# Attention phase of a float32 layer: scores of two blocks issued together, transposed probabilities kept in the score banks, and reordered first and last steps of the phase

## The reference, cut to what matters

```python
x = x + attn_ref(layernorm(x), mem, ...)        # x: 8192 rows of 256
x = x + ffn_ref(layernorm(x), ...)              # routed experts
# attn_ref, in front of each sequence 64 rows of mem:
q, k, v = x_in @ wq.T, x_in @ wk.T, x_in @ wv.T          # 4 heads of 64
mask = (j <= i) & (j > i - 128)                          # window of 128 keys
attn = softmax(where(mask, q @ k.T / 8, -1e30));  out_swa = (attn @ v) @ wo.T
grads = grad of 0.5 * sum((mlp(w1, b1, w2, b2, x_in) - out_swa) ** 2)
# one step on w1, b1, w2, b2; out = sigmoid(..) * out_swa + sigmoid(..) * mlp(new, x_in)
```

## Time and profile before

| | us |
| --- | --- |
| median of 3 runs | 2390.28 (2389.48 to 2391.47) |
| the profiled execution, device time | 2382.2 |
| its span in the profile | 2380.4 |
| PE busy | 2330.7 (98%) |
| DVE busy | 1691.1 (71%) |
| ACT busy | 1608.3 (68%) |
| POOL busy | 1394.6 (59%) |

### The profile page before, as it was taken

How to read it: one execution, slowest core, us unless ns; L and a number is a source line. 1 busy time by engine, 2 the same in 40 slices (tenths; PEclk the granted TensorE clock), 3 DMA queues, 4 the chain that set the end, 5 groups by cost and what they waited for, 6 DMA issues and landing times. The chain is left out here.

```text
span 2380.4 us, 39979 instructions
## 1 busy us (share of the span) xinstructions
PE 2330.7 (98%) x14822; PEld 2078.7 (87%) x14822; DVE 1691.1 (71%) x3666; ACT 1608.3 (68%) x2457; POOL 1394.6 (59%) x1000
## 2 busy tenths in 40 slices
PE   7999999899999999999999999999999999999998
PEld 6888888788888888888888978888888789999998
DVE  7787786666666666666666677777777867777776
ACT  4778878757777777777777647777777645554453
POOL 3566566656667766666666744666666553343433
PEclk9999999999999999999999999999999999999999
DMA  4222221442323322322233332332222165555551
GB/s 130 83 84 77 89 72 63 175 158 63 67 67 67 76 63 63 63 67 63 63 63 71 77 107 76 105 105 96 91 84 83 32 165 140 140 151 146 143 141 58
DMA packets 295394, 221.74 MB, mean 93 GB/s; under 512 B 189282, under 2 KB 262023, under 8 KB 295072
## 3 DMA queue, kind: packets, MB, share of 16 engines
q1 hardware_dynamic: 281376, 188.74, 29.3%
q0 software_dynamic: 13824, 30.44, 4.3%
HBM read 113.30 MB, written 72.12 MB: 78 GB/s over the span
## 5 line engine op out<-in xcount | busy, mean ns | idle before, releaser
L2742 ACT ACTIVATE e_hf<-e_ps_z,e_b 128x640 f32<-128x640 f32 x128 | 101.8, 795 | 211.9 <-PE e_ps_z L105 211.4
L2466 POOL TENSOR_TENSOR m_hl<-m_hf,m_hh 128x512 fp32r<-128x512 f32 x112 | 159.5, 1450 | 100.6 <-ACT m_hh L2067 100.4
L2870 POOL DMA_INDIRECT out<-e_ys,slot_token x80 | 83.2, 1040 | 216.6 <-DVE e_ys L2821 211.1
L105 PE MATMUL e_ps_y<-r_w_h,e_hl 128*128 128x256 f32 x640 | 180.7, 282 | 0.0
L105 PE MATMUL e_ps_y<-r_w_l,e_hh 128*128 128x256 f32 x640 | 179.3, 280 | 0.0
L105 PE MATMUL e_ps_y<-r_w_h,e_hh 128*128 128x256 f32 x640 | 179.0, 280 | 0.0
L914 POOL DMA_INDIRECT xbuf_d<-xn,scatter_rows x128 | 142.0, 1109 | 60.4 <-issue 35.4
L1650 POOL TENSOR_TENSOR halves_l<-hT_full,halves_h 128x512 fp32r<-128x512 f32 x120 | 153.5, 1301 | 38.7 <-ACT halves_h L1308 38.7
L771 POOL TENSOR_TENSOR prob<-prob,softmax_small 128x1024 f32<-128x1024 f32 x65 | 123.1, 1894 | 71.8 <-DVE softmax_small L689 71.8
L105 PE MATMUL e_ps_z<-slotsT_h,w_l 128*128 128x320 f32 x512 | 158.6, 310 | 0.7 <-DVE slotsT_l L2799 0.7
L105 PE MATMUL e_ps_z<-slotsT_l,w_h 128*128 128x320 f32 x512 | 158.5, 310 | 0.0
(11 more groups left out here) (359 smaller groups left out, 8961.2 us busy)
## 6 DMA issues: line engine op xcount, KB each, us to landing
shared_xT<-xT_d SPq DMA_DIRECT2D x64, 256.0 KB, 4.6
new_w1T<-in_W SPq DMA_DIRECT2D x16, 1024.0 KB
new_w2T<-in_W SPq DMA_DIRECT2D x16, 1024.0 KB, 5.7
xbuf_d<-new_w1T SPq DMA_DIRECT2D x16, 650.0 KB, 8.1
shared_x<-in_x SPq DMA_DIRECT2D x16, 512.0 KB, 4.1
xn_d<-xn SPq DMA_DIRECT2D x32, 256.0 KB, 2.5
xT_d<-shared_xT SPq DMA_DIRECT2D x32, 256.0 KB, 2.6
oT_d<-shared_oT SPq DMA_DIRECT2D x32, 256.0 KB, 2.6
```

What stands on the lines that cost most here:

```text
L105: i = e.matmul(out, a, b, start=first and not onto and n == 0, stop=last and n == len(terms) - 1, skip_group_check=onto)
L2466: e.tensor_tensor(hl[:, t, 0:N], hf[(HC * C + t) % NZ][:, 0:N], hh[:, t, 0:N], ALU.subtract).then_inc(*h_low(C, t))
L2742: e.activation(hf[(HC * i + t) % NHF][:].rearrange("p (s n) -> p s n", s=2), ps_z[t % 2][:, :, 0:HALF], ACTF.Relu, bias=b1[:, i % E, t:t + ...
L2870: e.indirect_dma_start(io["out"], bass.IndirectOffsetOnAxis(ap=token[i % 2][:, b:b + 1], axis=0), ys[:, b], None, bounds_check=NT - 1, oob ...
```

## The change

Six edits, all of order and place; the numbers computed are the same.

1. **Scores in pairs.** In an even turn PE issues `scores(a)` and `scores(a + 1)` one behind the other, in an odd turn none.
2. **Banks.** There are two sets of score banks, `ps_sets[g % 2]`, and the transposed probabilities of block g are written over the scores of block g + 2, in the same set; `ps_probT` is gone. So `transpose_p(g)` waits for the maxima of g + 2, and `scores(g)` for `rest_pt(g - 4)`.
3. **Order on ACT and DVE.** `soft(a)` goes ahead of the roundings and of `round_pt(a - 2)` (in turns 0, 4, 8, ... ahead of `round_pt` alone). DVE takes the maxima of an odd block in the even turn before it, and those of an even block at the end of the odd turn before it, behind `rest_pt`. In turns 0, 4, 8, ... the roundings of x come before the maxima of the odd block. POOL normalises `a - 1` ahead of the rests of x.
4. **Turns without early projections**: PE does `attend(a - 3)` first, then `transpose_p(a - 2)`.
5. **Opening.** The six projections of group 1 leave `opening()` and go, two in a turn, into turns -1, 0 and 1.
6. **The phase's end.** ACT rounds the first block of x for the gradient phase and loads the sigmoid's table ahead of the last output copies, DVE takes that block's rest; in the gradient phase the first seed goes ahead of `round_xT(0)`, the third block's x is rounded alone and early (`round_xT2`), and PE's first two products wait for no rest.

```diff
     G, j = a // GRP + 2, a % GRP
+    second = parts(1, 2 * a + 4) + parts(1, 2 * a + 5) if a < 2 else []
     if a < 0 or G >= NGRP:
-        return [], []
-    return parts(G, 2 * j) + (parts(G, 1) if j == 0 else []), parts(G, 2 * j + 1) if j else []
+        return [], second
+    return parts(G, 2 * j) + (parts(G, 1) if j == 0 else []), second + (parts(G, 2 * j + 1) if j else [])
...
         for n in range(2, 8):
-            out += parts(G, n)
+            out += parts(G, n) if G != 1 else []
...
-        ps_s = ps("ps_scores", [P, 2, 2, 2 * P])
-        ps_pt = ps("ps_probT", [P, 2, HEADS, P])
+        ps_sets = [ps(f"ps_scores{i}", [P, 2, 2, 2 * P]) for i in range(2)]
...
+        def scores_of(g):
+            return ps_sets[g % 2]
+
+        def probT_of(g):
+            return ps_sets[g % 2][:].rearrange("p b c (h q) -> p b (c h) q", q=P)
...
-                pe.wait_ge(*top_made.at(g - 1))
+                pe.wait_ge(*top_made.at(g - 2))
+                pe.wait_ge(*pt_low.at(g - 4))
+                ps_s = scores_of(g)
...
-                p = pr[g % NPR]
+                p, ps_pt = pr[g % NPR], probT_of(g)
                 pe.wait_ge(*prob_made.at(g))
-                pe.wait_ge(*pt_low.at(g - 1))
+                pe.wait_ge(*top_made.at(g + 2))
+                pe.wait_ge(*pt_low.at(g - 2))
...
-                if a in turns:
+                if a == MEM_BLOCK:
                     scores(a)
+                elif a % 2 == 0 and a in turns:
+                    scores(a)
+                    scores(a + 1)
                 for kind, *key in early:
                     do[kind](*key)
-                if a - 2 in turns:
+                if early and a - 2 in turns:
                     transpose_p(a - 2)
                 if a - 3 in turns and a - 3 < last:
                     attend(a - 3)
+                if not early and a - 2 in turns:
+                    transpose_p(a - 2)
...
+            def round_first():
+                act.wait_ge(*next_xT.at(0))
+                act.wait_ge(*score_done.at(NBLK - 9))
+                e.activation(firsth, shared.pair_xT(0)[:, :, 0:P], ACTF.Copy).then_inc(*first_high(0))
+
+            def load_sigmoid():
+                act.wait_ge(*half_set.at(0))
+                e.activation(spare[:], neg_half[:, 0:1], ACTF.Sigmoid)
...
+                if a % GRP and a in turns:
+                    soft(a)
                 for kind, *key in early:
                     do[kind](*key)
+                if a % GRP == 0 and a in turns:
+                    soft(a)
                 if a - 2 in turns:
                     round_pt(a - 2)
-                if a in turns:
-                    soft(a)
                 if a - 3 in turns and a - 3 < last:
                     copy_av(a - 3)
                 if a - 3 == last:
                     round_last_av()
+                    round_first()
+                    load_sigmoid()
                 for kind, *key in late + output_at(a):
                     do[kind](*key)
                 if a in w1_turns:
                     round_w1(w1_turns.index(a))
...
                 early, late = steps_at(a)
-                if a in turns:
+                if a == MEM_BLOCK:
                     maxima(a)
-                if a - 1 in turns:
+                if a % 2 and a - 1 in turns:
                     invert(a - 1)
-                for kind, *key in early:
-                    do[kind](*key)
+                if a % GRP == 0:
+                    for kind, *key in early:
+                        do[kind](*key)
+                if a % 2 == 0 and a + 1 in turns:
+                    maxima(a + 1)
+                if a % GRP:
+                    for kind, *key in early:
+                        do[kind](*key)
                 if a - 2 in turns:
                     rest_pt(a - 2)
-                for kind, *key in late:
-                    do[kind](*key)
+                if a % GRP != 1:
+                    for kind, *key in late:
+                        do[kind](*key)
                 if 0 <= a and G < NGRP and j == 0:
                     norm_stats(G, 0)
                     norm_stats(G, 1)
                 elif 0 <= a and G < NGRP and j < 3:
                     norm_apply(G, j - 1)
+                if a % 2 and a in turns:
+                    invert(a)
+                if a % 2 and a + 1 in turns:
+                    maxima(a + 1)
+                if a % GRP == 1:
+                    for kind, *key in late:
+                        do[kind](*key)
...
             rest_last_av()
+            dve.wait_ge(*first_high.at(0))
+            e.tensor_tensor(firstl, shared.pair_xT(0)[:, :, 0:P], firsth, ALU.subtract)
...
+                if a - 1 in turns:
+                    normalise(a - 1)
                 for kind, *key in early + late:
                     if kind == "x":
                         rest_x(*key)
-                if a - 1 in turns:
-                    normalise(a - 1)
...
+                h, l = (firsth, firstl) if g == 0 else (xTh[:, :, block[b]], xTl[:, :, block[b]])
                 for i, hc in enumerate(cols):
                     pe.wait_ge(*seeded.at(g, i))
-                    pe.wait_ge(*xT_low.at(p))
-                    matmul_split(e, bank("z", g, i)[:], [(xTh[:, k, block[b]], xTl[:, k, block[b]]) for k in range(KC)],
+                    if g:
+                        pe.wait_ge(*(xT2_low.at(0) if g == 2 else xT_low.at(p)))
+                    matmul_split(e, bank("z", g, i)[:], [(h[:, k], l[:, k]) for k in range(KC)],
...
+            seed(0)
             round_xT(0)
-            for n in range(ZBANKS):
+            for n in range(1, ZBANKS):
                 seed(n)
             forward(0, 0)
+            round_xT2()
             forward(0, 1, 0)
-            round_xT(1)
             seeds(0)
             forward(0, 1, 1)
+            round_xT(1)
```

More of the change, by code:

```diff
@@ L120, in w2T, with first_halves @@
         return [t[:, 0:HC * D].rearrange("p (k d) -> p k d", d=D) for t in self.keys]
+    def first_halves(self):
+        return [t[:, HC * D:HC * D + KC * P].rearrange("p (k t) -> p k t", k=KC) for t in self.keys]
     def pair_xT(self, i):
@@ L454, in attend_last @@
                 pe.wait_ge(*av_full.at(last - 1))
-                pe.wait_ge(*top_made.at(last))
+                pe.wait_ge(*pt_low.at(last - 1))
                 for kb in range(2):
@@ L466, in keep_busy @@
             def keep_busy(n):
-                pe.wait_ge(*top_made.at(last))
+                pe.wait_ge(*pt_low.at(last - 1))
                 ones = w["wq"][0]
                 for _ in range(n):
-                    e.matmul(ps_s[:, 0].rearrange("p a b -> p (a b)"), ones[:, 0, 0:P], ones[:].rearrange("p k d -> p (k d)"),
+                    e.matmul(ps_sets[0][:, 0].rearrange("p a b -> p (a b)"), ones[:, 0, 0:P], ones[:].rearrange("p k d -> p (k d)"),
                              start=True, stop=True)
@@ L539, in round_pt @@
                     return
-                e.activation(pth[g % 2][:], ps_pt[:], ACTF.Copy).then_inc(*pt_high(g))
+                e.activation(pth[g % 2][:], ps_pt, ACTF.Copy).then_inc(*pt_high(g))
             def soft(g):
@@ L605, in scalar @@
                     round_w2T(w2T_turns.index(a))
-            act.wait_ge(*half_set.at(0))
-            e.activation(spare[:], neg_half[:, 0:1], ACTF.Sigmoid)
         def vector(e):
@@ L1252, in round_xT, with round_xT2 @@
             def round_xT(p):
-                N = blocks_of(p) * P
+                t = slice(P if p < 2 else 0, blocks_of(p) * P)
                 act.wait_ge(*xT_ready(p))
                 act.wait_ge(*z_done.at(2 * p - 1, 1))
-                e.activation(xTh[:, :, 0:N], xT_f[p % 2][:, :, 0:N], ACTF.Copy).then_inc(*xT_high(p))
+                e.activation(xTh[:, :, t], xT_f[p % 2][:, :, t], ACTF.Copy).then_inc(*xT_high(p))
+            def round_xT2():
+                act.wait_ge(*xT_ready(1))
+                e.activation(xTh[:, :, 0:P], xT_f[1][:, :, 0:P], ACTF.Copy).then_inc(*xT2_high(0))
             def round_xn(p):
@@ L1423, in rest_xT, with rest_xT2 @@
             def rest_xT(p):
-                N = blocks_of(p) * P
+                t = slice(P if p < 2 else 0, blocks_of(p) * P)
                 dve.wait_ge(*xT_high.at(p))
-                e.tensor_tensor(xTl[:, :, 0:N], xT_f[p % 2][:, :, 0:N], xTh[:, :, 0:N], ALU.subtract).then_inc(*xT_low(p))
+                e.tensor_tensor(xTl[:, :, t], xT_f[p % 2][:, :, t], xTh[:, :, t], ALU.subtract).then_inc(*xT_low(p))
+            def rest_xT2():
+                dve.wait_ge(*xT2_high.at(0))
+                e.tensor_tensor(xTl[:, :, 0:P], xT_f[1][:, :, 0:P], xTh[:, :, 0:P], ALU.subtract).then_inc(*xT2_low(0))
             def rest_xn(p):
```

15 lines of the change are left out of this document (11 added, 4 removed).

## The result

The change makes the kernel slower: 2410.17 us (median of 6 runs, 2409.42 to 2412.65) against 2390.54 (6 runs, 2389.48 to 2391.47); ratio 1.0084, 95% interval [1.0072, 1.0096], which is +19.6 us. The prediction was 2389.8, range 2381.5 to 2397.5: the time lies outside it.

A forecast was written before the change was run, and what follows sets the result against it. PE was taken to bound nearly every slice, the order of three engines the last turns. Terms -11.2 + 2.8 - 2.4 + 10.4 + 3.2 - 3.3 = -0.5 gave 2389.8 us, range 2381.5 to 2397.5.

The forecast's parts named there:

- Pairs, -11.2: Blocks 0 to 55 on PE: scores directly behind scores spare 0.40 us a pair, 28 pairs, -11.2 us.
- New stalls in steady state, +2.8: Groups of four turns: PE newly waits about 0.23 us a group, 12 groups behind the opening, +2.8 us.
- ScalarE's row: Unbroken ACT work from turn 0, 9.6 us at least; turn 2's second scores wait for a low part, about 0.15 us.
- the x chain: Copy, rounding on DVE and two rests on POOL for x; ends about 0.1 us behind PE's need.
- rival (c): DVE's row without slack in turn 1 stalls every group by 0.8 us, giving 2396.6 us; chance 0.17.
- Opening, -2.4: First turns: old waits and slow clock worth 8.4 us get filled, new waits cost 6.0, so -2.4 us.
- Last turns, +10.4 and +3.2: From block 56 on: a chain of 10.9 us per two blocks costs +10.4; two falls of PE's clock +3.2.
- The phase's end, -3.3: End of attention and start of gradient phase: barrier 1.4 us sooner, two PE waits totalling 1.9 gone, -3.3 us.
- the third wait: Gradient phase's start: PE's 1.07 us wait for x's rest stays, since it hangs on transposes that move along.
- What would show it: Signs: block 56's scores at 389 (wrong outside 386 to 393), 33 us or more between maxima of 56 and 62, barrier about 1 later.

The follow-up runs named there:

- r13_split: r10_both with the two scores of an even turn taken apart, early projections between them, in blocks 0 to 55; ratio 0.9989 to the kernel before.
- r10_both: The change with x's first-half normalisation behind the maxima in turns 1, 5, 9, ... and last-turn scores one turn ahead, plain copies; ratio 0.9955 to the kernel before.
- r0_before: The kernel before with 135 transposing DMAs of two later phases turned into plain copies; ratio 1.0014 to the kernel before.
- r1_change: The change with 135 transposing DMAs of two later phases turned into plain copies; ratio 1.0085 to the kernel before.
- r4_last_turns: r1_change with the order of before on PE, ACT and VectorE in turns 56 to 67, both bank sets kept; ratio 1.0058 to the kernel before.
- r9_ahead: r1_change with another order in turns 57 to 67, PE issuing one block's scores one turn ahead; ratio 1.0011 to the kernel before.

## Why the prediction was wrong

**Pairs, -11.2: right, a little too large.** 1.62 for 1.80 us, no step inside over 0.13, and the edges gone. Against it, the x transposes behind a pair take 1.00 us, and behind a lone scores 0.93. Of the twelve groups eleven take 26.12 to 26.18 us, each with one stall of 1.17, and the last, without it, 24.93; before it was 25.57. That saves 0.6 a group, where pairs and small stalls together had 0.57 in the forecast. As a price by itself, with the second scores beside transposes, r13_split gives less: 6.9 to 8.1 us for all 28.

**New stalls in steady state, +2.8: this step failed.** It had 0.23 a group, from ScalarE's row and the x chain. The change has 26.05 - 24.77 = 1.3: eleven stalls of 1.17, 12.9 us, at a place to which the sum gave nothing, and the rest about as reckoned (r10_both, without the long one, has 0.3). Of the two small stalls the x chain's shows (GpSimd's second rest ends at 202.62, the q product starts at 202.68), ScalarE's only in the kernels with the bias on it. The place was in my text, as rival (c): the row of VectorE in turn 1 with no slack. But I gave the two normalising instructions the 0.73 us that they have in the kernel before, where GpSimd happened to stand still at that time (the rows at 189.93 above). A duration measured beside an idle neighbour was carried to a place beside a busy one. Rival (c) had the mechanism with 0.8 for 1.2, and 0.17 for a chance.

**Opening, -2.4: the new waits were right, the gain was not there.** I had 0.6, 1.25, 1.25 and 1.65 up to block 4's scores; the change has 0.49 (0.64 with the product's own end), 1.19, 1.18 and 1.65 to 1.72. Yet block 4 starts only 1.0 sooner (65.62 for 66.61). The old waits and the slow clock come to 6.9 there by the gaps between PE's runs of products, not 7.4; the scores of block -1, now alone between projections, cost an edge of 0.4 more; and the projections at 19 to 24 us, in the same order of instructions, began 0.2 later than in the profiled execution of before and ran at the slow pace until 23.1 us and not 20.6, which cost 1.1. This last part is chance: between r0_before and r1_change block 8 starts 2.4 us sooner (93.53 and 91.09), against 1.1 here and 4.0 in the forecast.

**Last turns, +10.4 and +3.2: right in kind, 5.5 too small.** From block 58's maxima to block 60's it is 13.49 us, against 10.9 in the forecast. By its own links: maxima to exponentials 2.58 (1.7), because the bias stood behind GpSimd; exponentials 2.10 (1.97); attention product to transposes 2.44 (1.45) and transposes to the high part 1.73 (1.13), both at 1.2 GHz; the four others within 0.04. The next pair takes 11.34, with no fall. So the chain was read rightly and the fall in this pair costs 1.6 as reckoned, but there were four and not two, and the bias added 0.9 at three places: 3.2 and 2.7, together 5.9, are about the 5.5. From block 56's maxima to block 62's it is 38.1 us, over the 33 that I had named. What the forecast did not have is that the order of before no longer fits the shared banks: put back as it was it gives only 7.5 of the 18 us (r4_last_turns), and with the scores one turn ahead all of them (r9_ahead).

**The phase's end, -3.3: right up to the third wait, 0.8 too much at the mark.** From the last output product to the seeds 1.63 us (472.54 to 474.17), before 2.84; the first two waits of the gradient phase are gone and the third, 1.07 at 486.71, stays: 12.54 us behind the seeds, before 14.68. So far -1.2 and -2.1, as forecast. Then a wait of 1.0 for VectorE comes that the kernel before has not, and at the mark it is -1.2 and -1.3.

**What would show it.** Block 56 begins at 404.34, outside the 386 to 393 that I had named; the seeds come 22 us later and not 1. The first of these signs pointed at steady state.

## What to carry to other kernels

A duration read from a trace holds for the neighbours it was read beside: before an order is moved, ask for each VectorE instruction on the new path whether GpSimd will be at work then, and bound its cost by GpSimd's longest instruction (here 1.90 us). If a tile is written over another one's, the writer inherits the wait for that one's reader: put at least one turn between them (here 52.2 us for 62.6 in the last turns). Look for busy time that grew with the same work (1691 to 1734 us); it is a wait that no list of waits shows.

## What the runs showed of the hardware

- A VectorE tensor-scalar instruction on 4 elements for each partition took from 0.17 to 1.08 us in the change; from 80 to 400 us each of the 37 that took over 0.25 ended with an instruction of GpSimd; making GpSimd wait brought x's normalisation from 752 to 406 ns and the kernel down by 12 us (10.6 at the mark).
- A change of form on PE costs less beside transposes (0.23 and 0.34 us for a lone scores in r13_split) than between 512-column products (0.40 in the kernel before).
- In the change PE's granted clock fell in the windows behind waits of 2.27 us and 3.53 (twice), did not behind one of 1.60, but did behind waits of 0.98, 0.98 and 1.82 us that end at 456.68, 461.58 and 465.95. In r4_last_turns it fell between 434 and 450 us, where no wait is over 1.7.
- At the start of the span the pace of the same 512-column products went from 0.43 to 0.23 us at 20.6 us in the profiled execution of before and at 23.1 in that of the change; the row of the granted clock reads 1.00 from 16 to 24 us in both.
